# Two weight tiles per instruction in the high/low split of a fused graph-network kernel

## What is computed

```python
h = relu(layernorm(x))
feat = concat([h[src], h[dst]], 1)
e = concat([relu(feat[a:b] @ W + bias) for the three kinds hh, oo, ho])
logit = e @ W_a + b_a
alpha = softmax of logit over the edges with the same dst
z = segment_sum(alpha * h[src], dst)
x = x + relu(concat([h, z], 1) @ (W_hn for rows 0:128, W_on for the others) + bias)
h = relu(layernorm(x))
x = x + A_norm @ (h @ W.T + b)          # A_norm: degree-normalised adjacency with self loops
```

## Time and profile before

| | us |
|---|---|
| median of 3 runs | 618.23 |
| lowest and highest of them | 616.69, 618.50 |
| the profiled execution, its own time | 613.89 |
| its span, first to last instruction | 612.1 |
| TensorE busy in it | 554.1 |
| VectorE busy | 449.3 |
| ScalarE busy | 295.1 |
| GpSimd busy | 185.9 |

### The profile page before, as it was taken

How to read it: one execution, slowest core, us unless ns; L and a number is a source line. 1 busy time by engine, 2 the same in 40 slices (tenths; PEclk the granted TensorE clock), 3 DMA queues, 4 the chain that set the end, 5 groups by cost and what they waited for, 6 DMA issues and landing times.

```text
span 612.1 us, 8188 instructions
## 1 busy us (share of the span) xinstructions
PE 554.1 (91%) x2356; PEld 406.4 (66%) x2361; DVE 449.3 (73%) x970; ACT 295.1 (48%) x471; POOL 185.9 (30%) x177
## 2 busy tenths in 40 slices
PE   1799999999797998898999997997998999999997
PEld 1688777777564676565666664564656887878885
DVE  6728247679596897999999977979547558888352
ACT  0822312112218989674847365849664455225200
POOL 3002200076255467455765566252000100000000
PEclk9999999999897999999899999889997999999999
DMA  8558664389999899999999999976763527502121
GB/s 322 175 176 304 234 240 150 125 214 382 346 281 329 264 322 322 329 304 320 361 350 340 309 341 339 282 204 186 273 209 126 198 88 269 169 0 90 49 87 51
DMA packets 56551, 144.71 MB, mean 236 GB/s; under 512 B 6339, under 2 KB 6467, under 8 KB 56515
## 3 DMA queue, kind: packets, MB, share of 16 engines
q0 software_dynamic: 22352, 81.28, 42.8%
q1 hardware_dynamic: 27072, 50.34, 24.1%
q10 hardware_dynamic: 7090, 12.65, 5.5%
HBM read 125.37 MB, written 18.87 MB: 236 GB/s over the span
## 4 chain that ended last, share of the span: by engine, by line
PE 42%; DVE 26%; DMA 17%; issue 6%; ACT 5%; POOL 3%; ACTq 0%; DVEq 0%; POOLq 0%
PE ps L711 25%; DMA gath<-tab_b,tabl_i 12%; DVE gath L994 5%; DVE ring_l L969 4%; PE ps L843 4%; PE ps L661 4%; PE ps L896 4%; PE ps L874 3%; DVE gath L989 3%; ACT onehot L531 2%; DVE onehot L1011 2%; DMA gath<-tab_a,tabl_i 2%; DVE stage L977 2%; DMA tab_b<-stage 1%; POOL gath L340 1%
## 5 line engine op out<-in xcount | busy, mean ns | idle before, releaser
L711 PE MATMUL ps<-ring_h,actT_h 128*128 128x512 f32 x504 | 217.5, 432 | 5.6 <-DVE actT_l L964 3.1
L711 PE MATMUL ps<-ring_h,actT_l 128*128 128x512 f32 x504 | 200.4, 398 | 0.0
L711 PE MATMUL ps<-ring_l,actT_h 128*128 128x512 f32 x504 | 199.8, 396 | 0.0
L531 ACT ACTIVATE onehot<-onehot,lgs 128x512 bf16<-128x512 bf16 x192 | 123.5, 712 | 64.4 <-DVE onehot L1011 41.6
L478 ACT CAST ring_h<-raw 128x512 fp32r<-128x512 f32 x160 | 95.1, 618 | 88.8 <-PE ps L711 67.9
L969 DVE TENSOR_TENSOR ring_l<-raw,ring_h 128x512 fp32r<-128x512 f32 x160 | 107.1, 684 | 25.7 <-ACT ring_h L478 23.5
L711 PEld LDWEIGHTS ps<-ring_h,actT_h 128*128 128x128 f32 x504 | 96.6, 192 | 37.6 <-DVE actT_l L964 3.3
L711 PEld LDWEIGHTS ps<-ring_h,actT_l 128*128 128x128 f32 x504 | 96.6, 192 | 21.7
L711 PEld LDWEIGHTS ps<-ring_l,actT_h 128*128 128x128 f32 x504 | 97.0, 192 | 19.7
L661 PE MATMUL ps<-onehot 128*128 128x512 bf16 x290 | 81.3, 391 | 29.2 <-ACT onehot L531 23.0
L994 DVE SCALAR_TENSOR_TENSOR gath<-gath,wa_b 128x1024 f32<-128x1024 f32 x64 | 78.3, 1223 | 24.5 <-DMA gath<-tab_b,tabl_i 23.3
(11 more groups left out here) (181 smaller groups left out, 540.1 us busy)
## 6 DMA issues: line engine op xcount, KB each, us to landing
raw<-in_L_gnn_W_ho_dram SPq DMA_DIRECT2D x32, 256.0 KB
raw<-in_L_gnn_W_oo_dram SPq DMA_DIRECT2D x32, 256.0 KB
raw<-in_L_gnn_W_hh_dram SPq DMA_DIRECT2D x32, 256.0 KB
raw<-in_L_gnn_W_on_dram SPq DMA_DIRECT2D x32, 256.0 KB
raw<-in_L_gnn_W_hn_dram SPq DMA_DIRECT2D x32, 256.0 KB
tab_a<-stage ACTq DMA_DIRECT2D x24, 256.0 KB
tab_b<-stage ACTq DMA_DIRECT2D x24, 256.0 KB
raw<-in_L_gnn_W_dram SPq DMA_DIRECT2D x16, 256.0 KB
```

The source lines that it names most:

```text
L531: ins = nc.scalar.mul(onehot[:, s, 1 + i, :], onehot[:, s, 1, :], lgs[:, i, q:q + 1])
L711: mm = nc.tensor.matmul(ps[:, first + m, :], w, v, start=(k == 0 and i == 0), stop=(k == KT - 1 and i == 2))
```

## The change

`round_w` and `low_w` do nothing for odd k. For even k they handle places k and k+1 of the ring in one instruction of 128x1024, wait for both loads and both free places, and signal by two. The loads stay one DMA per tile, and every call stays where it was.

```diff
             def round_w(q, k):
-                act.wait_ge(s_raw[k], (q if q < CH_EDGE + 2 else q + 2) * 16 + 16)
-                act.wait_ge(s_slot, q * KT + k + 1)
-                nc.scalar.copy(ring_h[:, k, :], raw[:, k % RAW, :]).then_inc(s_high, 1)
+
+                if k % 2:
+                    return
+                for i in (k, k + 1):
+                    act.wait_ge(s_raw[i], (q if q < CH_EDGE + 2 else q + 2) * 16 + 16)
+                act.wait_ge(s_slot, q * KT + k + 2)
+                nc.scalar.copy(ring_h[:, k:k + 2, :], raw[:, k:k + 2, :]).then_inc(s_high, 2)
...
             def low_w(q, k):
-                dve.wait_ge(s_high, q * KT + k + 1)
-                nc.vector.tensor_tensor(ring_l[:, k, :], raw[:, k % RAW, :], f32(ring_h[:, k, :]), ALU.subtract).then_inc(s_low, 1)
+
+                if k % 2:
+                    return
+                dve.wait_ge(s_high, q * KT + k + 2)
+                nc.vector.tensor_tensor(ring_l[:, k:k + 2, :], raw[:, k:k + 2, :], f32(ring_h[:, k:k + 2, :]), ALU.subtract).then_inc(s_low, 2)
```

## The result

The changed kernel takes 622.13 us (median of 19 runs, 618.22 to 625.88) against 618.10 (19 runs, 610.72 to 623.03) for the kernel before. The ratio is 1.0094, with a 95% interval of 1.0075 to 1.0113: slower by 5.8 us (4.6 to 7.0). The ratio compares runs on the same chips, which the two medians don't, and from here on a time given for a kernel's cost is its ratio's. The forecast was 2.9. The profiled execution took 625.31 us with a span of 623.3.

A forecast was written before the change was run, and what follows sets the result against it. No single bound: TensorE, then gathers together with VectorE, then TensorE. Terms 0.6 + 0.3 - 0.5 + 2.5 = 2.9 us gave 616.8 profiled and 618.2 + 2.9 = 621.1 timed; 8-in-10 range 616.8 to 623.5.

The forecast's parts named there:

- First tile: Start of TensorE: the wider first subtraction delays its first matmul, +0.6 us (0.5 to 0.7).
- Chunks 14 to 17: Trailing tiles: late low parts delay loads and TensorE, and VectorE's last low part passes its delay on, +2.5 us.
- (16,0): First tile of chunk 16: TensorE starts it 1.9 us later, through delays at (15,4) and (15,6).
- The price of a pair: Both edited lines: pairs last 1.06 and 1.22 us; a busy VectorE adds 1.14 and saves 0.06 a pair.
- half-clock rival: Near 506 us or before chunk 7: new TensorE waits halve its granted clock, +2.2 a spell, 623.3; chance 8%.
- The upper bound of 3.3: Chunks 14 to 17: +3.3 us if pairs' loads share the DMA engines and each second one lands 0.8 later.
- Middle, -0.2: Between start and tail: +0.3 at an odd step and -0.5 for saved VectorE overhead.
- TensorE's wait at (5,3): Middle, odd step: the paired subtraction adds 0.54 us to TensorE's 4.08 wait; half taken, +0.3 (0 to 0.55).
- The -0.5 for saved overhead: Middle, 220 to 390 us: some 24 pairs on busy VectorE save 0.5 us (0 to -2.5).
- twice the loss: Rival, near 506 us or before chunk 7: TensorE's clock halves for some tiles, +2.2 a spell, 623.3; chance 8%.
- no change: Rival: gathers swallow delays at the start and (5,3), the tail costs only 1.7; +1.5, 619.7; chance 27%.
- a gain through VectorE: Rival, middle: VectorE alone sets the pace, each pair saves 0.15 us; total -1.9, 616.3; chance 13%.

The follow-up runs named there:

- e1_tail_pairs: Against the kernel before: pairs only in chunks 14 to 19, single tiles in chunks 0 to 13; 622.33 us, ratio 1.0058.
- g2_pairs_where_covered: The change with the first two tiles and chunks 14 to 17 left single; 619.28 us, ratio 1.0028 to the kernel before.
- f1_first_pair_only: Against the kernel before: only tiles (0,0) and (0,1) paired, all else single; 618.54 us, ratio 1.0028.
- e4: Against the kernel before: only VectorE's subtractions paired, in all chunks, casts single; 640.81 us, ratio 1.0364.
- g3: Only subtractions paired, casts single, with ScalarE casting three tiles ahead instead of two; 622.62 us, ratio 1.0102 to the kernel before.
- g4: The changed kernel itself, unaltered, run again for a second trace; 624.49 us, ratio 1.0112 to the kernel before.
- h1: Against the kernel before: only the first two tiles paired, timed a second time; 618.58 us, ratio 1.0030.
- h4: The changed kernel itself, unaltered, timed beside three others on the same chip; 623.52 us, ratio 1.0118 to the kernel before.
- e3: Against the kernel before: only ScalarE's casts paired, in all chunks, subtractions single; 619.13 us, ratio 1.0031.
- f3: Against the kernel before: pairs only in chunks 14 and 15; 619.31 us, ratio 1.0026.
- f4: Against the kernel before: pairs only in chunks 16 and 17; 618.97 us, ratio 1.0043.
- g1: The change with only tiles (0,0) and (0,1) left single; 620.90 us, ratio 1.0061 to the kernel before.
- h2: The change with only the first pair left single, timed a second time; 623.72 us, ratio 1.0099 to the kernel before.
- f2: Against the kernel before: all tiles single, TensorE also waits for the low part of (0,1) before its first tile; 618.21 us, ratio 1.0017.
- e2: Against the kernel before: pairs only in chunks 0 to 13, singles from chunk 14 on; 619.54 us, ratio 1.0011.
- the fourth set: Four kernels timed together: first pair only, all but the first, first pair with chunks 14 to 19, the change; ratios 1.0030, 1.0099, 1.0087, 1.0118.

## Why the prediction was off

The direction and the mechanism in chunks 14 to 17 were right. The size was half of what was measured, 2.9 for 5.8. That the median of 622.13 lies inside 616.8 to 623.5 is luck: the same loss on the base of the forecast is 618.2 + 5.8 = 624.0, outside, and the two medians stand closer together than the ratio because they weren't taken on the same chips. Two terms of the sum failed. "First tile" put the granted clock at nothing, and "Chunks 14 to 17" priced the pair (16,0) and (16,1) at nothing of its own. By its steps:

- **The price of a pair** was right: 1.047 and 1.221 us, 1.13 added in a row. The Trainium skill (Perfetto Trace Analysis, Optimizing Scalar/DVE Operations) advises breaking an operation up where an unsaturated engine causes bubbles on another; the tail's 3.6 us in e1_tail_pairs agree with that half of the rule. Its other half, grouping where an engine is saturated, brought nothing that g2_pairs_where_covered can tell.
- **"First tile, +0.6" failed in the traces.** The delay of TensorE itself was right (0.63 in f1_first_pair_only, 0.81 after). What was missing is the granted clock behind it. Of the traces compared, seven have the first subtraction as a pair: the kernel after, e4, f1, g3, g4, h1 and h4. All have a spell of 3.4 or 6.8 us at half clock around or within 1.4 us behind the first matmul. Eight have a single subtraction there and TensorE not held back (the kernel before, e1, e3, f3, f4, g1, g2, h2); two of them have the spell, f4 and h2, both with a late first matmul by chance. The first bank copy comes at 45.1 on average in the seven, at 42.6 in the eight: 2.5 us, against 0.6. In timed runs the first pair costs 1.8 (0.3 to 3.3), and that interval holds 0.6. I had a half-clock rival, but put it at 506 us and chunk 7, where a wait is short, and not at the start, where TensorE has waited 3.08 us already.
- **"Chunks 14 to 17, +2.5" failed by its size.** It had the right chain and a term that was too small. Over the five traces with single tiles in the tail (before, f1, f2, g2, h1) the last low part ends at 29.2 behind t0, over the six with all pairs (after, e1, g1, g4, h2, h4) at 32.5: 3.25 more, and the time of e1_tail_pairs gives 3.6. From there to the end of the span these traces take 85.2 to 85.3 us (f2 86.7), so the delay is passed on in full, as forecast. The mis-sized term is (16,0). I had counted 1.9 from the delays of (15,4) and (15,6) and let its own pair hide behind them; f4_pairs_16_17 shows that it costs 1.8 by itself, because its cast waits for the second load and it and the subtraction last longer. In the kernel after the two together are 3.0. The low parts of (15,4) and (15,6) at 8.27 and 11.26 behind t0 are close to the 8.3 and 10.9 forecast. The upper bound of 3.3 did think of the second load. That its 0.8 met the 0.80 of f4_pairs_16_17 is chance, since no row stood behind it.
- **"Middle, -0.2"** can't be told from what was measured, though its parts didn't show. TensorE's wait at (5,3) went from 4.08 to 4.62 us, by the 0.54 forecast; in h4_change_third it was 3.32, so chance is larger than the step. The -0.5 for saved overhead didn't show. From the last bank copy of chunk 3 to the 58th edge tile seven traces with single tiles there (before, e1, f1, f2, f3, f4, h1) took 273.2 us on average, and six with pairs (after, g1, g2, g4, h2, h4) 273.5, from 272.6 to 274.2.

The sum of the kernels with one part each is 1.8 (0.3 to 3.3) for the start and 3.6 (1.7 to 5.5) for the tail: 5.4, against 5.8 measured. A second estimate uses the ratios of all eleven timed kernels that are made of start, middle and tail (after, e1, e2, f1, g1, g2, g4 and the four of the fourth set), takes the parts as adding up and weights each ratio by its interval. A least-squares fit then gives 1.3 (0.3 to 2.3) for the start, 0.6 (-0.6 to 1.9) for the middle and 4.1 (3.0 to 5.3) for the tail. The ratios of one set share their runs of the kernel before, so these intervals are somewhat too narrow. By this fit the tail was clearly priced too low, while the start's excess over 0.6 rests on the traces.

The rival "twice the loss" gave 623.3 from one more spell at half clock; the traces have such a spell, at the start and not where it was put. The rivals of no change and of a gain through VectorE fell. The first of these had a slip in its sum: it let the gathers swallow the delay at (5,3) and still added 0.3 for it, so it should have said 1.2 us and not 1.5.

What stays open: how often unprofiled runs of each kernel have the spell at the start. It is shown in traces only. That 1.8 is more than 0.6 speaks for it, but the interval holds 0.6, and f2_late_first_matmul speaks against it: it cost 1.0 us for a first matmul that was 1.4 late. A loss of the middle's own, of up to 2 us by the fit, isn't ruled out either.

## What to carry to other kernels

A wider instruction delays its first half wherever that is awaited, and it also waits for its second half's input: at a place where each load lands just in time, count the second load's landing (0.80 us at (16,0)), not only the longer durations (0.43 and 0.54). Before grouping, list the places where the grouped engine stands directly in front of the bound one. Here the other 63 of the 80 pairs earned nothing that shows, so the list decided. And if one of those places stands behind a wait of TensorE, look for its granted clock there: in these traces the longer wait came with a spell at half clock on top of the delay, and the forecast needs a term or a rival for it.

## What the hardware showed that was not expected

In f1_first_pair_only 0.63 us of lateness at TensorE's start took another 1.6 us of clock with it (2.25 at the first bank copy). TensorE waited 3.69 us there behind the transposes, where it waited 3.08 before, and ran at a granted clock of 0.50, 1.2 GHz, from 24 to 26 us; f2_late_first_matmul had waited 4.45. All eight compared traces with a wait of 3.69 us or more have the spell, and the six with 3.08 or 3.09 have none, g2 among them, though it started at 22.58. The length of the wait isn't the whole of it: f4 and h2 had the spell behind 2.97 and 2.99, after transposes that had themselves run slowly (6.45 and 6.43 us for the 32). The Trainium skill (TensorE: Matmul & The Clock Gate, Part 1) says that the clock falls when TensorE has stood idle and that the number of slow matmuls at the start differs between runs of one kernel. These traces agree with both, with the spell behind the longer waits and lengths of 3.4 and 6.8 us in executions of the same changed kernel (after and g4_change_again).
